# Attention operands of 48 and 50 rows without zeroed rows, and one merged order of the attention's steps

## What is computed

```
Q, K, V = proj(Wq, bq), proj(Wk, bk), proj(Wv, bv)       # 16 heads of 16
Q = _apply_rope(Q, cos, sin)
K = _apply_rope(K, cos, sin)
scores = jnp.einsum('bhqd,bhkd->bhqk', Q, K) * (1.0 / math.sqrt(D_K))
scores = jnp.where(causal[None, None], scores, -jnp.inf)
probs = jax.nn.softmax(scores, axis=-1)
att = jnp.einsum('bhqk,bhkd->bhqd', probs, V)
att = att.transpose(0, 2, 1, 3).reshape(b, s, d)
return jnp.einsum('bsd,ed->bse', att, Wo) + bo
```

## Time and profile before

| | |
|---|---|
| time, median of 3 runs | 1047.74 us (1046.58 to 1052.08) |
| the profiled execution | 1046.52 us, span 1044.9 us |
| mean granted TensorE clock | 0.816 of 2.4 GHz |
| PE busy | 744.3 us (71%), 3738 matmuls |
| PEld busy | 518.4 us (50%) |
| DVE busy | 624.1 us (60%) |
| ACT busy | 372.0 us (36%) |
| POOL busy | 340.5 us (33%) |

### The profile page before, as it was taken

How to read it: one execution, slowest core, us unless ns; L and a number is a source line. 1 busy time by engine, 2 the same in 40 slices (tenths; PEclk the granted TensorE clock), 3 DMA queues, 4 the chain that set the end, 5 groups by cost and what they waited for, 6 DMA issues and landing times. The chain is left out here.

```text
span 1044.9 us, 11081 instructions
## 1 busy us (share of the span) xinstructions
PE 744.3 (71%) x3738; PEld 518.4 (50%) x3738; DVE 624.1 (60%) x1019; ACT 372.0 (36%) x749; POOL 340.5 (33%) x372
## 2 busy tenths in 40 slices
PE   2817568777888869678913937859958888776980
PEld 2716345435444358667813724525535555475870
DVE  4996454354656048563434838668977989763232
ACT  3401132322545523203302474557634455220330
POOL 1294132210111212060042005437736677315005
PEclk9958767656988769688965967979979999968995
DMA  4702902212000050125530000000023000013444
GB/s 157 257 0 30 112 1 43 34 18 32 2 2 1 1 221 21 32 80 180 167 112 20 1 0 0 1 1 1 0 83 160 0 1 1 1 37 117 137 135 120
DMA packets 31990, 60.60 MB, mean 58 GB/s; under 512 B 3152, under 2 KB 22992, under 8 KB 30368
## 3 DMA queue, kind: packets, MB, share of 16 engines
q1 hardware_dynamic: 28864, 51.51, 17.3%
q0 software_dynamic: 3072, 8.39, 2.6%
HBM read 35.45 MB, written 17.43 MB: 51 GB/s over the span
## 5 line engine op out<-in xcount | busy, mean ns | idle before, releaser
L1195 PE MATMUL PS<-FB,C 128*128 128x512 f32 x256 | 134.0, 623 | 1.2 <-DVE FB L1828 1.2
L1288 ACT ACTIVATE FA<-PS 128x512 f32<-128x512 f32 (+3 forms) x192 | 83.2, 490 | 107.4 <-PE PS L970 106.6
L1910 POOL TENSOR_SCALAR_AFFINE_SELECT FA<-FA 128x128 f32<-128x128 f32 x128 | 37.1, 298 | 179.2 <-ACT FA L1288 177.6
L1947 POOL TENSOR_TENSOR FB<-FB,RBF 128x512 f32<-128x512 f32 x51 | 65.8, 1290 | 71.9 <-DVE FB L1819 71.9
L442 PE MATMUL PS<-C,FB 128*128 128x128 f32 x250 | 45.2, 305 | 56.0 <-DVE FB L1485 38.6
L1928 POOL DMA_INDIRECT FB<-GY,FB x32 | 30.7, 960 | 134.9 <-DMA GY<-FB 125.9
L970 PE MATMUL PS<-RA 64*128 64x512 f32 (+3 forms) x192 | 67.2, 487 | 9.7 <-ACT FA L1288 5.0
L942 PE MATMUL PS<-RA 64*128 64x128 f32 (+3 forms) x288 | 66.6, 447 | 10.2 <-DVE FA L1549 4.5
L442 PEld LDWEIGHTS PS<-C,FB 128*128 128x128 f32 x250 | 35.7, 158 | 68.1 <-DVE FB L1485 39.6
L1938 POOL TENSOR_TENSOR FB<-WE,FB 128x512 f32<-128x512 f32 x32 | 43.0, 1343 | 58.9 <-ACT FB L1384 58.9
L1093 PE MATMUL PS<-WE,FB 128*128 x248 | 61.3, 391 | 0.0
(11 more groups left out here) (260 smaller groups left out, 1735.0 us busy)
## 6 DMA issues: line engine op xcount, KB each, us to landing
WE<-in_wr SPq DMA_DIRECT2D x8, 1536.0 KB, 11.4
FB<-GX SPq DMA_DIRECT2D x14, 512.0 KB, 4.7
GY<-FB SPq DMA_DIRECT2D x14, 512.0 KB, 3.2
RA<-RA SPq DMA_DIRECT2D x48, 128.0 KB, 5.6
GX<-FA SPq DMA_DIRECT2D x1, 3968.0 KB, 14.1
FA<-in_w SPq DMA_DIRECT2D x2, 1024.0 KB, 7.2
FA<-in_qkvo SPq DMA_DIRECT2D x1, 1536.0 KB, 18.8
FB<-in_we SPq DMA_DIRECT2D x4, 384.0 KB, 3.4
```

The lines of the kernel that those rows point to most:

```text
L1195: pe.matmul(bank(m), ident, shc[k % 4], start=n == 0, stop=n == DN - 1).then_inc(*yad.inc(ch, n, m))
L1288: act.activation(PT[n % 12][:, c0:], bank(4 + ring_no[(x, *a)] % 3)[:, c0:], ACT.Exp, scale=0.25).then_inc(*exd.inc(*a))
L1947: pool.tensor_tensor(shc[k % 4], sh[k % 5], Cs[(stc.no[ch, n] - 1) % 2], ALU.mult).then_inc(*cma.inc(ch, n, m))
```

## The change

1. The operands are closed up: the third pair of parts moves from rows 48 to 63 to rows 32 to 47, the maxima and the -1 to rows 48 and 49. Raw scores use 48 rows (0 to 47 of each half), scores less maximum 50. So nothing has to be zero: the zero rows of KT and QT, the step `mzero` with its DMAs and waits, and the four memsets go. The -1 come from a small tile `NEG` (128x64, set by POOL at the very start) by two DMAs of SP, issued in step `qld` behind the rope load; PE waits for them before the first `sc`.
2. `attention_steps` gives the chunk-0 projections and values in the old order and hands everything else to `by_load`: streams for the heads of all eight groups, for the two late projections of q, for the chunk-1 norm, projections and values (`later`), and for the maxima of all eight groups. `by_load` keeps a time for each engine, gives each step one engine and a duration (`busy_with`), and takes next the step that can start first by these; `needs` holds a group's first score behind its maxima (4 us), spreads `later` over the maxima of chunk 0, and holds the late q projections behind the scores that still read the old rows.
3. `fin` of the last group of chunk 0, `attT(0)` and the four `oproj` of chunk 0 move into the heads of group (1, 0).

In the order that comes out, two `stat` steps stand among the maxima of the first group and `nrm` right behind its `mtt`; each late `pj` stands with its `rp1` among scores and its `rp2` some steps later. Between the last context of chunk 0 and its `raw` on one side and the first score of chunk 1 on the other stand seven `off`, `mx` and `mtt` of group (1, 0), then one `diag` and three `off` of group (1, 1). `mtt` of (1, 1) stands behind the `raw` of (1, 0), followed by one `diag` and three `off` of (1, 2) and then the first score of (1, 1); the transposes of the last two groups stand inside the heads of the group before.

```
 def maxima_steps(ch, g):
-    if ch:
-        yield [("mzero", ch, g)]
...
-            if kt == LAG and g:
-                yield [("fin", ch, g - 1)]
+            if kt == LAG and (ch or g):
+                yield [("fin", *((ch, g - 1) if g else (0, 3)))]
+            if ch and g == 0 and kt == LAG + 1:
+                yield [("attT", 0)]
+            if ch and g == 0 and LAG + 2 <= kt < LAG + 2 + TC:
+                yield [("oproj", 0, kt - LAG - 2)]
...
-def output_steps(ch):
-    yield [("fin", ch, 3)]
-    yield [("attT", ch)]
-    for i in range(TC):
-        yield [("oproj", ch, i)]
+def busy_with(step):
+    x, *a = step
+    if x == "sc":
+        return "act", 0.2 + 0.0008 * (CH - max(0, (a[2] - a[0] * TC) * P))
+    if x == "off":
+        h, per, _, w = next(q for q in off_groups(a[0], a[2]) if q[0] == a[3])
+        return "dve", 0.2 + 0.001 * per * w
+    if x in ("pv", "pj"):
+        return "pe", {"pv": 0.8, "pj": 2.6}[x]
+    return "dve", {"diag": 1.3, "mx": 0.7, "mtt": 0.1, "rp1": 1.5, "rp2": 0.7, "vj": 1.5, "raw": 0.7, "fin": 0.8, "attT": 1.3, "oproj": 0.5, "stat": 1.2, "nrm": 0.8, "xn": 0.7}.get(x, 0.1)
+def by_load(streams, needs):
+    streams, free, at, out = [list(s) for s in streams], {}, {}, []
+    while any(streams):
+        best = None
+        for k, s in enumerate(streams):
+            if s:
+                need = [n for x in s[0] for n in needs.get(x, [])]
+                if all(n in at for n, _ in need):
+                    t = max([free.get(busy_with(s[0][0])[0], 0.0)] + [at[n] + late for n, late in need])
+                    if best is None or t < best[0]:
+                        best = (t, k)
+        t, k = best
+        seg = streams[k].pop(0)
+        for x in seg:
+            e, n = busy_with(x)
+            t = max(t, free.get(e, 0.0)) + n
+            free[e] = at[x] = t
+        out.append(seg)
+    return out
 def attention_steps():
     q0, q1, k0, k1 = ("q", 0), ("q", 1), ("k", 0), ("k", 1)
-    yield [("xbo", 0), ("mzero", 0, 0)]
+    yield [("xbo", 0), ("mfloor",)]
     yield from project_steps(0, [q0, k0, q1, k1])
     yield from values_steps(0)
-    yield from maxima_steps(0, 0)
-    yield from weave((chain(maxima_steps(0, 1), norm_steps(1, 1), [[("xbo", 1)]]), 1), (heads_steps(0, 0), 1))
-    yield from weave((chain(maxima_steps(0, 2), project_steps(1, [k0, k1]), values_steps(1)), 1), (heads_steps(0, 1), 1))
-    yield from weave((chain(maxima_steps(0, 3), project_steps(1, [q0])), 0.7), (heads_steps(0, 2), 1))
-    yield from weave((chain(heads_steps(0, 3), project_steps(1, [q1]), output_steps(0)), 1), (maxima_steps(1, 0), 0.8))
-    for g in range(3):
-        yield from weave((maxima_steps(1, g + 1), 0.65), (heads_steps(1, g), 1))
-    yield from heads_steps(1, 3)
-    yield from output_steps(1)
+    def turned(w):
+        yield [("pj", 1, *w), ("rp1", 1, *w)]
+        yield [("rp2", 1, *w)]
+    groups = [(ch, g) for ch in range(NCH) for g in range(4)]
+    maxima = list(chain(*[maxima_steps(*k) for k in groups]))
+    heads = list(chain(*[heads_steps(*k) for k in groups]))
+    norm = list(norm_steps(1, 1))
+    norm[-3:] = [[x for seg in norm[-3:] for x in seg]]
+    later = norm + [[("xbo", 1)]] + list(chain(turned(k0), turned(k1), values_steps(1)))
+    needs = {}
+    for ch, g in groups:
+        needs["sc", ch, g, 0, 0] = [(("mtt", ch, g), 4.0)]
+    first = maxima.index([("diag", 1, 0, 0)])
+    for i, seg in enumerate(later):
+        needs[seg[0]] = [(maxima[(i + 1) * (first - 8) // len(later)][0], 0.0)]
+    for u in range(2):
+        needs["pj", 1, "q", u] = [(("sc", 0, 2 * u + 1, 1, 3), 0.0), (later[-1][0], 0.0)]
+        needs["rp2", 1, "q", u] = [(("sc", 0, 2 * u + 1, TC - 1, 3), 0.0)]
+        needs["diag", 1, 2 * u, 0] = [(("rp2", 1, "q", u), 6.0)]
+    yield from by_load([heads, turned(q0), turned(q1), later, maxima], needs)
+    yield [("fin", 1, 3)]
+    yield [("attT", 1)]
+    for i in range(TC):
+        yield [("oproj", 1, i)]
...
-                elif x == "mzero":
-                    ch, g = a
-                    if ch == 0:
-                        sp.wait_ge(*kset.at())
-                        sp.wait_ge(*xad.at(0, 1))
-                        qpad.inc()
-                        for r in (32, 96):
-                            for o, n in ((0, 14), (14, 2)):
-                                sp.dma_start(QT[r + o:r + o + n, :, :].bitcast(F), KT[34:34 + n, 0:4, :].bitcast(F)).then_inc(qpad.sem, 16)
-                    else:
-                        sp.wait_ge(*scs.at(0, g, TC - 1, 3))
-                        mzd.inc(ch, g)
-                        for r in (32, 96):
-                            sp.dma_start(QT[r:r + 2, 2 * g:2 * g + 2, :].bitcast(F), KT[34:36, 0, :].bitcast(F)).then_inc(mzd.sem, 16)
+                    sp.wait_ge(*pset.at("minus"))
+                    kset.inc()
+                    for r in range(2):
+                        sp.dma_start(KT[64 * r + 48:64 * r + 50, :, :].bitcast(F), NEG[0:2, :].bitcast(F).unsqueeze(1).broadcast_to([2, 128, 64])).then_inc(kset.sem, 16)
                 elif x == "rp2":
                     ch, w, u = a
                     hi, lo = stage[(rpl.no[ch, w, u] - 1) % 2]
                         sp.wait_ge(*scs.at(0, 2 * u + 1, TC - 1, 3))
                     sp.wait_ge(*rpl.at(ch, w, u))
                     plc[w, u].inc(ch)
-                    for src, at in ((hi, 0), (hi if w == "k" else lo, 16), (lo if w == "k" else hi, 48)):
+                    for src, at in ((hi, 0), (hi if w == "k" else lo, 16), (lo if w == "k" else hi, 32)):
                         for r in range(2):
                             sp.dma_start(to[64 * r + at:64 * r + at + 16, :, :].bitcast(F), src[64 * r:64 * r + 64, :].bitcast(F)).then_inc(plc[w, u].sem, 16)
                 elif x == "mtt":
...
-                        if ch:
-                            pe.wait_ge(*mzd.at(ch, g))
-                            pe.wait_ge(*kset.at())
-                            pe.wait_ge(*qpad.at())
-                        r = slice(64 * (hh % 2), 64 * (hh % 2) + 64)
+                        r = slice(64 * (hh % 2), 64 * (hh % 2) + 48)
...
+                        if ch == g == 0:
+                            pe.wait_ge(*kset.at())
+                    r = slice(64 * (hh % 2), 64 * (hh % 2) + 50)
                     pe.matmul(bk[:, c0:CH], KT[r, 2 * g + hh // 2, kt * P:kt * P + P], QT[r, 2 * g + hh // 2, c0:CH],
...
+                    pool.memset(NEG[:, :].bitcast(F), -1.0).then_inc(*pset.inc("minus"))
...
-                    pool.wait_ge(*vset.at())
-                    for r in (32, 96):
-                        pool.memset(KT[r:r + 16, :, :].bitcast(F), 0.0).then_inc(*p_own.inc())
-                        pool.wait_ge(*p_own.at())
-                    for r in (32, 96):
-                        last = pool.memset(KT[r:r + 2, :, :].bitcast(F), -1.0)
-                        last.then_inc(*(p_own if r == 32 else kset).inc())
-                        pool.wait_ge(*(p_own if r == 32 else kset).at())
```

## The result

The changed kernel takes 1008.0 us (median of 4 runs, 1005.2 to 1009.8) against 1047.2 us of the kernel before beside it: a ratio of 0.961, 95% interval 0.957 to 0.965. The profiled execution takes 1006.24 us, with a span of 1004.6 us. The forecast was 987.5 us with a range of 964 to 1014: the time is inside the range, the sign is right, and 18.7 us of the expected 59 are missing in the profiled execution.

The account below looks back on a forecast made before the run. No engine is full overall: POOL's memsets hold up FFN 0, in-order queues set attention's chunk 0, and PE nears its limit in chunk 1. From 1046.5 us, -26.5 - 29 - 3.5 = -59 gives 987.5, range 964 to 1014.

Parts of the forecast that it names:

- The memsets: Second half of FFN 0: removing four POOL memsets takes off 26.5 us, bounds -24 and -26.5.
- The -1 rows by DMA: Two early 64 KB DMAs, hidden before the first score that reads them: cost 0, uncovered 6 to 17 us.
- the zero rows' wait: Attention, chunk 0: PE's 6.18 us wait for a DMA goes, counted within chunk 0's gain.
- 48 and 50 rows: Scores and maxima read these instead of 64: costed at nothing, bounds 0 and a gain of 13 us.
- Chunk 0: Attention, first part: the new order takes 109 us against 137.78, -29; bounds 97 (-41) and 137 (nothing).
- Chunk 1: Attention, second part: 104 us, -3.5, with PE at density 0.89 and clock 0.90; bounds 91 and 112.
- the first rival: Attention: in-order queues just move their waits, so it gains only 0 to 15 us: 1005 to 1020; chance 0.20.
- The rise of the clock: Attention: a denser order holds a granted clock of 0.93, -79.5 in all, 967 us; chance 0.16.
- The chains before the scores: Attention: maxima-to-first-score chains stand bare before seven more groups, costing 35.4 us: 1055 in all; chance 0.03.
- the pairing: Attention: score pairs run one after the other, losing 22 us at full clock, 44 at half: 1010 to 1033; chance 0.04.

Follow-up runs that it names:

- the best: The changed kernel with chunk 0's output projection moved to the last group of chunk 1 and 64 rows in the heads' scores: 989.9 us, 0.946 of the kernel before.

## Why the prediction was right, and where it was 20 us too good

- **The memsets: right.** Forecast -26.5, -25.0 in the profiled execution, -26.7 in the one with 64 rows (66.53). The difference between the two is PE's clock in that stretch (0.84 and 1.00 over 57.25 to 68.20), not POOL's addition, though during it a DVE subtraction took 2.75 us and not 0.69. The Trainium skill (SBUF — State Buffer, SBUF: two separate sides) says that DVE and POOL share a pair of ports, and that an instruction that needs the pair holds it to its end. The trace agrees: the subtraction ended at 62.07, 0.56 us behind the end of POOL's addition of 2.48 us.
- **The -1 rows by DMA and the zero rows' wait: right.** No wait for either is left.
- **48 and 50 rows: a step that failed.** I costed the edit at nothing and bounded it by a gain only. At equal clock nothing is what it costs: stretches of the same order agree within 0.1 us. But against the 64-row kernel, which adds four DMAs to the rows, the changed one is 6.9 us slower beside it (0.963 and 0.956), and about 1% in the first pair, each beside the kernel before (0.961 and 0.952), at a lower mean clock (medians 0.811 and 0.826 beside each other). The sign was outside my bounds.
- **Chunk 0: right in kind, mis-sized by 5 us.** The first maxima took 15.77 us (14.7 forecast). Behind them 98.26 us instead of 94: PE's 81.52 us of work at a density of 0.83, where I took 85.3 at 0.87. The clock, 0.71, was inside the 0.63 to 0.75 assumed. The order alone gave 20 us by itself.
- **Chunk 1: wrong sign, by 9 us, and 1 us outside the bound of 112.** The density was better than assumed (0.93, not 0.89). The term that failed is the clock: 0.74, not the 0.90 that I took without a row for it. It was low in two places. In the last group (0.56, before 0.80) ACT is the full engine at the start, PE is thin, the clock falls and does not come back. The runs with extra matmuls and with the output projection put there show that the clock and not the order made this group long; but the thin start was there before the change as well, so why the clock came back then and not now is not shown. In the first stretch the clock was 0.73, before 0.93. No run explains that: from the last copy of chunk 0 to the first of chunk 1 it was 0.68 to 0.76 in every kernel of the new order, the best included, and 0.79 before. Group 2's gain of 6.5 us made up for most of the last group's loss. The Trainium skill (TensorE: Matmul & The Clock Gate, Part 1) says the clock follows how busy the array has been. The fall behind the thin start agrees; that it then stays at 0.50 to the end of a group with PE recorded busy 26.51 of 28.05 us does not agree with the busy time as the profile models it.
- **The rivals.** Luck had a part: 1008 us also lies in the range of the first rival, only the memsets (1005 to 1020), so the total alone does not tell it from the forecast. What does is the attention, which gained 18.2 us (245.3 to 227.1) where that rival gave it at most 15, and the order alone, worth 2% with all memsets kept. The rise of the clock was real but not had: the best kernels hold 1.00 in two or three groups of chunk 1 and come to 989, not 967, as chunk 0 stays near 0.7. The chains before the scores did not stand bare (PE waits 9.1 us in all, six times, for joined maxima, and 1.0 us for a placed one), and the pairing was not lost (50 and 64 rows take equal time at equal clock). The sums of the prediction come out but for small slips: the slow bound of the pairing rival is 987.5 + 44 = 1031.5, not 1033.

Added up, -25.0 + 1.5 - 23.75 + 5.55 + 1.4 = -40.3. The three positive terms lie in stretches that were granted less than before: 0.88 and not 0.94 from FFN 0 to the first maxima, 0.74 and not 0.84 in chunk 1, 0.50 and not 0.70 in the output projection behind it.

Open is why the kernel with fewer rows is granted a lower clock. With 64 rows in the heads' scores alone the added rows are zeros, so nothing computed explains it; but the 64-row kernels also send those zeros by four early DMAs, whose share was not separated. A rival stands beside the rows: the moment at which a stretch begins. The changed kernel's two profiles start the attention at 95.96 and 94.33 us, and their group 2 took 24.48 us at 0.86 and 26.73 at 0.74; the 64-row kernel's two start at 92.71 and 94.45, with 24.45 and 26.74. No run held that moment fixed. Open too is how far the clock varies in the old order: there the memsets' 25 us became 8 us with fewer rows and, with 64, 7 to 31 in single executions against a median of 1048.1.

## What to carry to other kernels

Where the granted clock is below 1, cost an edit in PE time at both levels, and ask of each stretch which engine is full at its start: if it isn't PE, the clock may fall there and stay down. Work that can go anywhere (here a projection) can be worth more in such a thin start than where its inputs come ready; here it was some 12 us. Taking away rows or work that seem free can cost time through the clock, so time the small edit by itself, several runs each, beside the kernel it came from.

## What the runs showed that I had not expected

Sixteen matmuls whose result no one reads made the kernel 7.8 us faster (1001.5 against 1009.3). Reading 64 rows and not 48 and 50, most of the added ones zeros sent by four more DMAs, made it 6.9 us faster (1002.4 against 1009.3), with equal durations at equal clock. And one group of 100 matmuls in the same order took 28.0 us at a mean clock of 0.56 to 0.58 and 22.6 at 0.77; the spread of one kernel's times, 1016.9 to 1040.8 us at mean clocks of 0.825 to 0.801, goes the same way.
